# Order of the weighing in a software-pipelined attention kernel (four chained transformer layers, one core)

## The reference

```
s = einsum('bqhd,bkhd->bhqk', q, k) * scale
a = softmax(where(mask, s, min), axis=-1)
out = einsum('bhqk,bkhd->bqhd', a, v) @ wo
```

## Time and profile before

| | |
|---|---|
| runs | 1069.88, 1067.48 and 4715.3 us; median 1069.88 us |
| profiled execution | 1063.98 us, span 1061.8 us, mean granted TensorE clock 0.952 |
| chain that ended last | PE 68%, DVE 14%, issue 8%, POOL 7%, ACT 1%, SP's queue 1% |
| PE busy | 971.6 us (91%) |
| DVE busy | 749.7 us (71%) |
| ACT busy | 623.6 us (59%) |
| POOL busy | 616.5 us (58%) |
| waits of ACT's copy to `k_high` (L1683) for the DMA into `q_ring` | 6.5 us in all, 10 times of 40 |
| jobs of phase one | about 62 to 344 us |
| jobs of phase two | about 617 to 999 us |

### The profile page before, as it was taken

One profiled execution on the slowest core, in us unless ns is written; L12 is line 12 of the kernel. 1 busy time (PEld: TensorE's weight loads), 2 busy tenths in 40 slices (PEclk: granted clock), 3 DMA queues, 4 the chain that ended last, 5 costly groups with the idle time before them and its releaser, 6 DMA issues.

```text
span 1061.8 us, 32084 instructions
## 1 busy us (share of the span) xinstructions
PE 971.6 (91%) x13009; PEld 670.9 (63%) x13009; DVE 749.7 (71%) x1852; ACT 623.6 (59%) x938; POOL 616.5 (58%) x739
## 2 busy tenths in 40 slices
PE   7898898998889999999999988888999998888998
PEld 5455565666566776676776655655666666566676
DVE  7767888777875444677787768877898766776421
ACT  2144455577767555545554567775677677775752
POOL 6657888576874332111113779776778655685520
PEclk9569999999997999999999989998999999997999
DMA  6613333434332102000000133333334333333011
GB/s 215 219 65 112 120 108 107 133 107 134 125 120 74 41 30 98 9 10 7 7 7 19 59 116 107 123 107 103 131 112 145 116 125 119 110 98 121 7 40 40
DMA packets 101459, 96.89 MB, mean 91 GB/s; under 512 B 11632, under 2 KB 93808, under 8 KB 100928
## 3 DMA queue, kind: packets, MB, share of 16 engines
q1 hardware_dynamic: 101312, 94.84, 26.9%
HBM read 18.77 MB, written 2.15 MB: 20 GB/s over the span
## 4 chain that ended last, share of the span: by engine, by line
PE 68%; DVE 14%; issue 8%; POOL 7%; ACT 1%; SPq 1%; DMA 0%; POOLq 0%; DVEq 0%; ACTq 0%
PE weighed L725 13%; DVE negmax L1242 8%; PE row_scores L658 8%; PE scores L921 6%; PE weighed L748 5%; PE scores L613 4%; PE row_scores L921 3%; PE quads L620 3%; POOL kblk_r L1952 3%; PE quads L594 2%; PE row_scores L738 2%; PE scores L738 2%; PE quads L605 2%; PE row_scores L634 2%; PE weighed L938 2%
## 5 line engine op out<-in xcount | busy, mean ns | idle before, releaser
L1242 DVE TENSOR_REDUCE negmax<-row_scores 128x8 f32<-128x616 f32 (+1 forms) x312 | 298.5, 957 | 101.4 <-PE row_scores L658 74.4
L1758 ACT ACTIVATE p<-scores 128x1024 f32<-128x1024 f32 (+1 forms) x253 | 253.1, 1019 | 123.4 <-PE scores L710 87.7
L1952 POOL TENSOR_TENSOR kblk_r<-work,pack_const 128x308 fp32r<-128x308 f32 (+1 forms) x160 | 133.6, 836 | 113.0 <-PE row_scores L658 92.1
L658 PE MATMUL row_scores<-kblk_r,qr 32*128 32x308 f32 (+1 forms) x624 | 145.5, 457 | 52.4 <-DVE negmax L1242 42.4
L725 PE MATMUL weighed<-p,v 77*32 77x128 f32 (+1 forms) x5120 | 184.4, 288 | 1.8 <-DVE nat L1258 1.3
L725 PEld LDWEIGHTS weighed<-p,v 77*32 77x32 f32 (+1 forms) x5120 | 137.9, 114 | 36.1 <-issue 27.2
L658 PEld LDWEIGHTS row_scores<-kblk_r,qr 32*128 32x128 f32 x624 | 63.9, 191 | 130.2 <-issue 84.6
L695 PE MATMUL scores<-q_ring,k_ring 32*77 32x128 f32 (+1 forms) x2512 | 123.0, 256 | 4.4 <-ACT shared L1695 1.7
L695 PEld LDWEIGHTS scores<-q_ring,k_ring 32*77 32x77 f32 (+1 forms) x2512 | 100.0, 167 | 7.9 <-ACT shared L1695 1.9
L1258 DVE STREAM_TRANSPOSE nat<-weighed 128x256 f32<-128x256 f32 x160 | 70.9, 443 | 41.8 <-PE weighed L725 37.1
L710 PE MATMUL scores<-nblk,select 32*77 32x512 bf16 (+1 forms) x628 | 93.1, 396 | 0.0
(11 more groups left out here) (334 smaller groups left out, 1958.1 us busy)
## 6 DMA issues: line engine op xcount, KB each, us to landing
q_ring<-work SPq DMA_DIRECT2D x160, 128.0 KB, 2.1
q_ring<-qr SPq DMA_DIRECT2D x160, 128.0 KB, 2.1
k_ring<-k_high SPq DMA_DIRECT2D x64, 128.0 KB, 2.1
k_ring<-work SPq DMA_DIRECT2D x64, 128.0 KB, 2.1
k_ring<-k_high SPq DMA_DIRECT2D x96, 77.0 KB, 2.0
k_ring<-work SPq DMA_DIRECT2D x96, 77.0 KB, 2.0
shared<-gates_hbm SPq DMA_DIRECT2D x24, 256.0 KB, 3.1
shared<-in_ctx_tok SPq DMA_DIRECT2D x15, 154.0 KB
```

The source lines that it names most:

```text
L658: mm = e.matmul(row_banks(n, h)[:, i, 0:cols], qr[q % 3][at, s * S:(s + 1) * S], kblk_r[n % 2][at, 0:cols], start=layer.mask is None or ma ...
L1242: e.tensor_reduce(negmax[q % 2][:, 2 * h:2 * h + 2, s * NJ:(s + 1) * NJ], row_banks(n, h)[:, :, 0:NJ * nk].rearrange("p g (j k) -> p g j k ...
L1758: e.activation(p[n % 2][0:nk, 8 * h:8 * h + 8, :], score_banks(n, h)[0:nk].rearrange("p g (j q) -> p (g j) q", j=NJ), ACT.Exp, bias=hide, ...
L1952: e.tensor_tensor(kblk_r[n % 2][:, 0:NJ * nk].rearrange("p (j k) -> p j k", j=NJ), k_of[q % 2][:, s * nk:(s + 1) * nk].unsqueeze(1).to_bro ...
```

## The change

Four things, none of which alters what is computed.

1. TensorE: `weigh(t - 1)` comes right behind the subtractions of job t (in l0 behind the second mask's addition) and ahead of `rows(t + 6, 0)`. `quad_ahead` is gone and all projections follow the row scores.
2. TensorE: `turn_max(q)` waits in addition for the transposition of the last weighed values (`nat_done`).
3. VectorE: `turn_blocks(t - 1)` comes ahead of `row_max(t + 6, 0)`; it stood behind it and behind other work of the slot.
4. POOL: the splits of a quad move from slot cl 3 to the next slot (cl 0), behind its `normalise`; only a phase's first quad is split where it was.

```
@@ turn_max
                 w.wait_ge(act_setup, ACT_AT["ident_bf"])
+                if q:
+                    w.wait_ge(nat_done, 4 * q - (2 if layer_of(q - 1).mask == "qk" else 1))
@@ TensorE, attention
-                def is_wide(t):
-                def quad_ahead(qi, cl):
...
                         shift(t, 0)
                         shift(t, 1)
-                    if is_wide(t):
-                        quad_ahead(qi, cl)
-                    if phase == 1 and t in (4 * lo - 2, 4 * lo - 1):
-                        keep_busy(4, av_bank[:, 0:128])
-                    if t + 6 in jobs:
-                        rows(t + 6, 0)
                     if masked:
-                        mask_rows(t + 6, 0, False)
                         mask_scores(t, 1)
                         if cl == 3 and qi + 1 in quads:
                             w.wait_ge(nblk_done, qi + 2)
-                    if masked or is_wide(t) and cl == 2:
-                        quad_work(t, qi, cl)
-                        if t - 1 in jobs:
-                            weigh(t - 1)
-                    else:
...
+                    if t - 1 in jobs:
+                        weigh(t - 1)
+                    if t + 6 in jobs:
+                        rows(t + 6, 0)
+                        mask_rows(t + 6, 0, False)
...
+                    if not masked and cl == 3 and qi + 1 in quads:
+                        turn_max(qi + 1)
+                    quad_work(t, qi, cl)
@@ VectorE, attention
+                    if t - 1 in jobs:
+                        turn_blocks(t - 1)
                     if t + 6 in jobs:
                         row_max(t + 6, 0)
...
-                    if masked and cl == 2 and qi + 1 in quads:
-                        w.wait_ge(negmax_turned, qi + 2)
-                    if t - 1 in jobs:
-                        turn_blocks(t - 1)
@@ POOL, attention
                         normalise(t - 2)
-                    if cl == 3 and qi + 2 in quads:
-                        split_q(qi + 2)
-                        split_k(qi + 2)
+                    if t == 4 * lo - 5:
+                        split_q(lo)
+                        split_k(lo)
+                    if cl == 0 and qi + 1 in quads and qi + 1 != lo:
+                        split_q(qi + 1)
+                        split_k(qi + 1)
```

More of the change, by code:

```diff
@@ L786, in quads_read @@
                             w.wait_ge(q_done, qi + 3 - NB + 1)
-                def is_wide(t):
-                    return t in jobs and layer_of(t // QUAD).nk == S
-                def quad_ahead(qi, cl):
[L794 to L801, removed]
                 def quad_work(t, qi, cl):
@@ L815, in quad_work @@
                             quads_read(t - back)
-                    rest = slice(2 if is_wide(t) else 0, QUAD)
                     if cl == 0 and qi + 2 in quads and t != -2 * QUAD:
-                        project_k(qi + 2, rest)
+                        project_k(qi + 2)
                     if cl == 1 and qi + 3 in quads and layer_of(qi + 3).name == "l3c":
@@ L822, in quad_work @@
                         turn_normed(norm_at[t])
-                    if cl == 2 and qi - 2 in quads and not is_wide(t):
+                    if cl == 2 and qi - 2 in quads:
                         if qi >= hi:
@@ L826, in quad_work @@
                         project_out(qi - 2)
-                    if cl == 3 and qi + 3 in quads and not (is_wide(t) and layer_of(qi).rope):
-                        project_q(qi + 3, rest)
+                    if cl == 3 and qi + 3 in quads:
+                        project_q(qi + 3)
                 for t in range(4 * lo + first, end):
@@ L857, in attention @@
                             w.wait_ge(nblk_done, qi + 2)
-                    if masked or is_wide(t) and cl == 2:
-                        quad_work(t, qi, cl)
-                        if t - 1 in jobs:
-                            weigh(t - 1)
-                    else:
-                        if t == 4 * hi:
-                            first_layer(phase, 0, hi, range(2))
-                        if t - 1 in jobs:
[L866 to L873, removed]
+                    if phase == 1 and t in (4 * lo - 2, 4 * lo - 1):
+                        keep_busy(4, av_bank[:, 0:128])
+                    if t == 4 * hi:
+                        first_layer(phase, 0, hi, range(2))
+                    if t - 1 in jobs:
[3 more added lines that the diff above has]
+                        mask_rows(t + 6, 0, False)
+                    if t in (-6, -4, -3):
+                        keep_busy(3, scores[:, 0, 0:128])
+                    if not masked and cl == 3 and qi + 1 in quads:
+                        turn_max(qi + 1)
+                    quad_work(t, qi, cl)
                     if masked and cl == 2 and qi + 1 in quads:
```

## The result

The changed kernel takes 1188.32 us (median of 4 runs, 1174.7 to 1199.29) against 1069.38 for the kernel before in runs on the same chip: a ratio of 1.108, interval 1.095 to 1.121. The forecast was 1107, its range ended at 1133. The medians are over all runs; ratios and their intervals leave out a run that is over 1.5% above the fastest of its kernel, which puts this loss at 115 us where the medians put it at 119. It is slower, as forecast, and the ring that was forecast does close; but the loss is three times the 37 that were expected, and most of it goes by a way that the sum left out.

A forecast was written before the change was run, and what follows sets the result against it. The kernel was taken as bound by its order of work, with a slackless DMA ring in narrow layers. Steady quads 6 + 17 + 9 and border quads 5.5 add 37.5 us to 1063.98: 1101.5, as median 1107, range 1077 to 1133.

The forecast's parts named there:

- the ring: Split, 16 DMAs, copy to `k_high`, second exponential, `exact`, through two quads: 33.3 us per two narrow periods, 16.65 a quad.
- the 37 that were expected: Whole loss summed: l0 6, l0c, l2 and l3c 17, l3s 9, border quads 5.5, together 37.5 us.
- 15.75 us round, as long as a narrow quad: Trace reading from one low-key landing to the next, taken to show no slack for the copy in narrow layers.
- A uniform stall: ACT's wait for the DMAs spread over nearly every quad, about 1.5 us of stall in one place per quad.
- The missing 4.1 us are waited by ACT: Narrow quads: DMAs need 13.0 us, the moved splits leave 8.9; ACT waits, then the next quad's `exact`.
- The sum above leaves the clock as it is: TensorE's clock: the predicted gaps were held short enough not to lower it, so nothing was added.
- The second rival: TensorE falls to 1.2 GHz for a third of each narrow quad: about 20 us more, 1127; chance 0.18.
- The norm behind the splits: POOL's norm steps end 2.6 us into cl 1, TensorE wants them at 2.3: nothing that a period sees.
- The new order of weighing: TensorE and VectorE: narrow quads of work fall to 15.0 us (bounds 14.0 to 15.8); l0 20.6, l3s 16.7.
- The first rival: The DMAs are hidden and the ring never closes: narrow quads 15.0, median 1065, not slower; chance 0.17.
- the third: Rival: work between shortens more, narrow quads of work 14.0, two periods 32.3, time about 1090; chance 0.15.

The follow-up runs named there:

- e3: The changed kernel with eight dummy 128x128 matmuls on TensorE ahead of each quad's first score matmuls: 1117.5 us, ratio 1.048 to the kernel before.
- e5: e1 with seven dummy matmuls per narrow quad on TensorE: 1070.8 us, ratio 0.996 to the kernel before.
- e9: The kernel before with only the DMAs of the high parts issued first, ahead of the splits' low parts: 1056.7 us, ratio 0.988.
- e10: The changed kernel with only the DMAs of the high parts issued first: 1088.7 us, ratio 1.020 to the kernel before.
- e8: e1 with the DMAs of the high parts issued first, only the low ones waiting for the splits: 1047.4 us, ratio 0.978 to the kernel before.
- e1: The changed kernel with only its fourth part undone, splits back in cl 3: 1083.0 us, ratio 1.016 to the kernel before.
- e2: The kernel before with only the fourth part of the change, splits moved to cl 0: 1185.6 us, ratio at least 1.084.

## Why the prediction was off

**What bounds, and the ring: right.** The second ring that the earlier trace rows showed is the one that closed. Its arithmetic, two periods = a quad of work + split + DMAs + copy and exponential, was met in e3 to within half a microsecond a quad (in l0 0.8), and in l3s of after as a sum: 16.2 + 20.2 = 36.4 for two quads against 2 x 18.15 = 36.3. Term by term, from `exact` at 856.41 to the `exact` at 893.17, it is 17.5 for the quad of work (16.7 forecast; part of it runs at the lower clock, and at full clock it is 16.2), 4.8 to the end of the split (4.9), 12.8 for the DMAs (13.1) and 1.6 for copy and exponential (1.6). So the three short terms were right, and that the sum came out to 0.1 is luck: a quad of work taken too long, and one made longer by the clock. One reading was weaker than it looked: "15.75 us round, as long as a narrow quad" is the time from one quad's low keys to the next one's and equals the period whatever the ring does. What spoke for a ring without slack was that the copy starts 0.1 us behind the last landing (919.09). e5 fits it (15.3 to 16.1 in most narrow quads, with the copy waiting), but e9, with the ring open, has narrow quads of 15.3 to 16.0 as well: in the kernel before, work and ring were about equally long.

**A uniform stall: wrong.** The ring fixes the sum of two quads, not each. I wrote "The missing 4.1 us are waited by ACT", and that a stall does not add up every quad; this is what the trace shows, in most of phase two 3 to 5 us in every second quad. Then I divided it and let "about 1.5 us of stall stand in one place per quad". That longer single stalls are dearer by the clock is likely but not shown: the clock also fell at a pause of 1.43 us (l0, 150.2).

**"The sum above leaves the clock as it is": the step that failed.** With the clock held by fillers the change costs 48 us (e3) against the 37.5 of my sum; by stages l0 is 18 us longer (6 forecast), l0c 10 (4), l2 3 (6), l3s 15 (9) and l3c 6 (6). With the clock free it costs 119. So 71 us, 60% of the loss, go through the clock (64 us and 56% by the ratios), and I had put this term at nothing. An upper bound comes from the clocks: after has some 220 us more at 1.2 GHz than before, and if everything waited for TensorE in all of them, half of that, 110 us, would be lost. The second rival named this and asked for a clock under 0.93; it was 0.863. But it was priced at 20 us: a third of each narrow quad at half clock, l0 left out. The four stages that lost 20 us or more ran at 0.78 or 0.79, that is some 42% of their time at 1.2 GHz (half speed for a share s gives 1 - s/2), l0 too.

The Trainium skill, "TensorE: Matmul & The Clock Gate", section "Why this matters for your kernels", warns of idle gaps between bursts of matmuls. I had taken it that gaps as short as these fall outside its rule. The trace disagrees with that reading: around 852 to 856 TensorE was still busy 2.05 of 4 us, its longest pause was 2.20 us, and the next window had 0.60; in l0 it was busy 3.04 of 4 us, paused 1.43 us, and the next window had 0.53. Other pauses ahead of `exact` reached 4.4 us, which I had not forecast.

**The norm behind the splits: wrong.** I had the norm's steps end 0.3 us after TensorE wants them and called it "nothing that a period sees", with numbers from narrow slots. In l0 POOL has rotation and two wide splits ahead of them, and TensorE waits 1.43 us at 150.47; in l2, a narrow stage, it waits too, 5 times in after, 5.2 us in all. The forecast for l0 was 6 us, the loss 30. The norm's waits make some 10 us of it, if they cost here what they did in e10. Another 14 lie in l0's first two quads (32.9 and 28.2 us against 23.7 and 23.3), where the clock is low until 116 us and no wait for the norm or the DMAs is seen; their cause stays open.

**The new order of weighing: right in size, but it could not show.** Narrow quads of work were taken as 15.0; with the ring open and the clock up they are 14.0 to 15.1 (e8), l3s 16.2 instead of the 16.7 I took, l0 20.5 (20.6). The ring stood at nearly 15.75, so the gain turned into waits for the DMA (e1: 27.8 us in place of 6.5) and a lower clock. The first rival (1065, the DMAs hidden) is refuted by the copy's waits, the third was half right: quads of l3c are 14.0 to 14.7 of work where it had 14.0, but with the clock held the time is 1117 (e3), and not 1090.

Of the 119 us: the splits' place makes all of it (e2, and 105 of it by e1), some 64 to 71 by the clock. How the rest divides among the ring, the fillers' own time in e3 and l0's norm is not told apart to better than some 20 us, since a stall in one place changes the clock in the next, and a single stretch of low clock in one execution can cost that much (l2 of e8).

## What to carry to other kernels

Before work moves along a slot, look for a single buffer whose copy stands in an in-order engine ahead of something that TensorE needs, and add up split, issue, landing and copy against the period; where they are equal, neither earlier nor faster work brings much until that sum is cut, and the order in which DMAs are issued is a cheap place to cut it. A ring that reaches through two periods can give its stall to every second one, whole: look at the longest pause, not the mean. Then price a pause on TensorE with the clock behind it, also one of a microsecond and a half; here that made the change two to three times as dear. And before a stage's time is put down to an edit, look whether a long stretch of low clock lies in it.

## What the runs showed of the hardware

- A pause of 2.20 us, with TensorE busy 2.05 of 4 us, was followed by a window at 0.60 and the same 32 matmuls at 1.93 us instead of 1.08. With eight matmuls in that place (2.05 us busy) the clock of l2 and l3s was 1.00 all along.
- A pause of 1.43 us, with TensorE busy 3.04 of 4 us, was followed by a window at 0.53.
- A busy TensorE did not always get its clock back: in e8 it was busy 53.55 of 54 us at 0.50 throughout.
- Work that computes nothing made a kernel 6% faster (e3 against after), and one with more waiting in all.
- Sixteen DMAs issued one by one by one queue took 11.4 us; issuing the first high parts 2.3 us earlier (e8, l3s), with as many DMAs and bytes, gave 1.2% to the kernel before and 8% to after (1088.7 against 1188.3).
